# Small attention layers: v kept on the chip, first groups loaded during the in-projection, out-projection with tokens on partitions

## The reference

```python
# layer 0
x = x + _L0_attn_a_ref(_layernorm(x), Wq, Wk, Wv, Wo, W_down_kv, W_up_k, W_up_v)
    latent_kv = (x @ Wk + x @ Wv) @ W_down_kv
    qh, kh, vh = heads(x @ Wq), heads(latent_kv @ W_up_k), heads(latent_kv @ W_up_v)
    scores = clip(einsum('bhqd,bhkd->bhqk', qh, kh) * scale, -1e4, 1e4) * decay
    attn = softmax(clip(scores, -1e4, 1e4))
    return einsum('bhqk,bhkd->bhqd', attn, vh) (heads joined) @ Wo
# layer 4
x = x + _L1_attn_a_ref(_layernorm(x), Wqkv, Wout, Wpos, coeffs)
    logits = einsum('bihd,bjhd->bhij', q, k) * 8 ** -0.5 + pos_bias
    return einsum('bhij,bjhd->bihd', softmax(logits), v) (heads joined) @ Wout.T
```

## Time and profile before

| | us |
|---|---|
| runs, median of 3 (lowest to highest) | 4288.15 (4287.07 to 4292.68) |
| profiled execution, its own time | 4286.97 |
| span of the profiled execution | 4285.2 |
| layer 0: in-projection, attention, out-projection, statistics | 24.3 to 98.8, to 813.5, to 841.1, to 853.5 |
| layer 4: the same | 3004.6 to 3076.5, to 3644.8, to 3673.4, to 3685.7 |

### The profile page before, as it was taken

One profiled execution on the slowest core, in us unless ns is written; L12 is line 12 of the kernel. 1 busy time (PEld: TensorE's weight loads), 2 busy tenths in 40 slices (PEclk: granted clock), 3 DMA queues, 4 the chain that ended last, 5 costly groups with the idle time before them and its releaser, 6 DMA issues. The chain is left out here.

```text
span 4285.2 us, 58306 instructions
## 1 busy us (share of the span) xinstructions
PE 3440.0 (80%) x18432; PEld 2108.1 (49%) x18432; DVE 3112.8 (73%) x7125; ACT 2445.8 (57%) x4454; POOL 1239.0 (29%) x855
## 2 busy tenths in 40 slices
PE   5788888687946999999999978793499999657736
PEld 2455555365733555555555536572366666433314
DVE  3899999656864777777777745685388887569986
ACT  2788888535722656556565534572299999322203
POOL 0000000034421566666566654341000000025520
PEclk9899999878976999999999988896799999778868
DMA  5333332212436666666766611342634342100000
GB/s 184 60 62 62 62 51 35 37 42 102 143 97 81 86 87 89 85 85 87 90 85 86 84 23 46 112 142 67 189 45 61 60 64 31 26 18 8 5 29 26
DMA packets 285571, 303.79 MB, mean 71 GB/s; under 512 B 97951, under 2 KB 187487, under 8 KB 285140
## 3 DMA queue, kind: packets, MB, share of 16 engines
q1 hardware_dynamic: 275540, 279.07, 37.0%
q0 software_dynamic: 9728, 20.99, 1.4%
HBM read 122.30 MB, written 75.96 MB: 46 GB/s over the span
## 5 line engine op out<-in xcount | busy, mean ns | idle before, releaser
L1118 DVE TENSOR_REDUCE at_b_top<-ps 128x1 f32<-128x512 f32 x1024 | 661.9, 680 | 356.9 <-PE ps L878 356.2
L1007 ACT ACTIVATE at_b_e<-ps 128x512 f32<-128x512 f32 x1024 | 583.6, 598 | 474.2 <-PE ps L884 461.2
L550 ACT ACTIVATE at_a_e<-at_a_logits,at_a_neg_top 128x512 f32<-128x512 f32 x1024 | 656.1, 716 | 156.1 <-DVE at_a_neg_top L610 155.0
L777 POOL TENSOR_TENSOR at_b_e_pair<-at_b_e 128x1024 f32<-128x1024 f32 x256 | 603.8, 2380 | 402.5 <-PE ps L906 400.0
L474 PE MATMUL ps<-at_a_k,at_a_q 96*128 96x512 f32 x1024 | 476.3, 491 | 187.4 <-DVE at_a_clipped L578 118.3
L878 PE MATMUL ps<-at_b_k,at_b_q 96*128 96x512 f32 x1024 | 502.0, 494 | 40.2 <-DMA at_b_k<-at_b_k_hi 37.9
L543 ACT ACTIVATE at_a_eT<-ps 128x512 f32<-128x512 f32 x896 | 461.9, 589 | 0.4
L884 PE MATMUL ps<-at_b_q,at_b_k 98*128 98x512 f32 x1024 | 427.2, 418 | 19.0 <-ACT at_b_e L1007 18.6
L606 DVE CUSTOM_DVE_ANT_0 at_a_logits<-ps,at_a_strip 128x512 f32<-128x512 f32 x512 | 340.3, 688 | 110.7 <-issue 33.1
L474 PEld LDWEIGHTS ps<-at_a_k,at_a_q 96*128 96x128 f32 x1024 | 184.7, 190 | 399.8 <-DVE at_a_clipped L578 208.8
L578 DVE TENSOR_SCALAR at_a_clipped<-ps 128x512 f32<-128x512 f32 x512 | 351.2, 686 | 39.1 <-PE ps L474 38.0
(11 more groups left out here) (333 smaller groups left out, 6451.5 us busy)
## 6 DMA issues: line engine op xcount, KB each, us to landing
moe_stage<-in_moe_w SPq DMA_DIRECT2D x46, 768.0 KB
at_b_q<-at_b_q_hi SPq DMA_DIRECT2D x128, 256.0 KB, 5.2
at_b_k<-at_b_k_hi SPq DMA_DIRECT2D x128, 256.0 KB, 7.7
v<-in_a_va SPq DMA_DIRECT2D x64, 256.0 KB, 3.6
at_a_v<-v SPq DMA_DIRECT2D x64, 256.0 KB, 7.2
at_b_q<-at_b_q_lo SPq DMA_DIRECT2D x64, 256.0 KB, 7.6
at_b_k<-at_b_k_lo SPq DMA_DIRECT2D x64, 256.0 KB, 8.0
slot_rows<-empty_slots SPq DMA_DIRECT2D x44, 288.0 KB, 7.0
```

What stands on the lines that cost most here:

```text
L550: act.activation(e[:, j, qb, :], logits[:, j % 2, qb, :], ACT.Exp, bias=neg_top[:, j % 2, qb:qb + 1]).then_inc(exp_done, 1)
L777: pool.tensor_tensor(e_pair[:, j, :, :], e[r][:, j, 0:2, :], e[r][:, j, 2:4, :], ALU.add).then_inc(pair_done, 1)
L1007: act.activation(e[r][:, j, b, :], g.ps[:, ST_BANK + b % 2, :], ACT.Exp).then_inc(exp_done, 1)
L1118: dve.tensor_reduce(top[:, t, j, qb:qb + 1], g.ps[:, bank, :], AX_X, ALU.max).then_inc(max_done, 1)
```

## The change

- A new class `SmallBuffers` holds `q4`, `k4`, the decay strip or the bias strips, and a new `v_all` (v of all batches, 8 x 4 x 128 columns on each partition, unpadded). It lives across in-projection and attention. Its semaphores are not cleared.
- In-projection: `va` with its zeros and ones is gone; DVE copies v into `v_all`; SP stores no v. POOL zeroes `q4` and `k4` here. After the weights SP loads the decay strip (layer 0) or the four bias strips (layer 4). After the stores of batches 5 and 6 it loads the q and k pieces of attention groups 1 and 2.
- Attention: POOL sets the padding of the four `v4`, then copies, for each group, 16 x 8 columns of `v_all` into `v4` (once the product of the group four before is done). SP starts with the loads of group 3. The first bias strips aren't loaded here.
- Out-projection: a ring of four for o; w is loaded after the first batch's o; PE multiplies with the turned o as the stationary side, in four pieces, so that the result has tokens on partitions; the copy L1662 and the turn L1642 are gone. DVE takes `bn_stats` of batch n - 1 after the add of batch n. The phase is followed by a `row_stats` phase that only has the `bn_aggr` and the short steps, and the next layer's own is skipped.

```diff
+class SmallBuffers:
+    def __init__(self, nc, stack, sems, name, decay):
...
+        self.v_all = sb("v_all", [P, B, TB, DM])
+    def zero(self, pool):
+        for r in range(2):
+            pool.memset(self.q4[r][:].bitcast(F32), 0.0).then_inc(self.zeroed, 1)
+            pool.memset(self.k4[r][:].bitcast(F32), 0.0).then_inc(self.zeroed, 1)
+    def load_stacks(self, sp, g, r, batch, heads):
+        for row, dq, dk in ((0, g.q_hi8, g.k_hi8), (32, g.q_hi8, g.k_lo8), (64, g.q_lo8, g.k_hi8)):
+            for dst, src in ((self.q4[r], dq), (self.k4[r], dk)):
+                sp.dma_start(dst[row:row + 8].bitcast(F32),
...
 def project_small(nc, g, name, scale, latent, weights, ahead):
...
+            @block.gpsimd
+            def _(pool):
+                ahead.zero(pool)
...
+                if latent:
+                    sp.dma_start(ahead.decay_strip[:], g.decay).then_inc(ahead.decay_loaded, 16)
+                else:
+                    for j in range(HG):
+                        ahead.load_strip(sp, g, j, 0)
...
-                        sp.wait_ge(v_done, n)
-                        settle(sp, sp_settled)
-                        for hg in range(4):
-                            sp.dma_start(g.v8[bass.ds((n - 1) * 4 + hg, 1)].rearrange("a (t p) n -> p (a t) n", p=P),
...
+                        if n in (5, 6):
+                            if n == 5:
+                                sp.wait_ge(ahead.zeroed, 4)
+                            sp.wait_ge(stored[n % 2], 16 * 4)
+                            ahead.load_stacks(sp, g, n % 2, n - 5, 0)
...
-                for r in range(2):
-                    dve.memset(va[r][:], 0.0).then_inc(ones_set, 1)
-                dve.wait_ge(ones_set, 2)
-                for r in range(2):
-                    dve.memset(va[r][:, :, :, 8:9], 1.0).then_inc(ones_set, 1)
-                dve.wait_ge(ones_set, 4)
...
-                        dve.tensor_copy(va[r][:, :, :, 0:8], bank_v.rearrange("p (t h d) -> p t h d", t=TB, d=8)
+                        dve.tensor_copy(ahead.v_all[:, n - 1], bank_v.rearrange("p (t c) -> p t c", t=TB)
                                         ).then_inc(v_done, 1)
...
 def attend_small(nc, g, name, decay, ahead):
...
-                for r in range(2):
-                    pool.memset(q4[r][:].bitcast(F32), 0.0).then_inc(zeroed, 1)
-                    pool.memset(k4[r][:].bitcast(F32), 0.0).then_inc(zeroed, 1)
+                for r in range(4):
+                    pool.memset(v4[r][:], 0.0).then_inc(v_set, 1)
...
+                        wait(pool, pv_done, n - 4)
+                        pool.tensor_copy(v4[n % 4][:].rearrange("p t (h d) -> p t h d", d=32)[:, :, :, 0:8],
+                                         ahead.v_all[:, batch, :, heads * 32:heads * 32 + 32].rearrange(
+                                             "p t (h d) -> p t h d", d=8)).then_inc(v_spread, 1)
...
-                if decay:
-                    sp.dma_start(decay_strip[:], g.decay).then_inc(decay_loaded, 16)
-                sp.wait_ge(zeroed, 4)
...
-                        wait(sp, pv_done, n - 4)
-                        settle(sp, sp_settled)
-                        sp.dma_start(v4[rv][:], item(g.v8, batch * 4 + heads + 1).rearrange("a (t p) n -> p (a t) n", p=P)
-                                     ).then_inc(v_loaded[rv], 16)
-                        if not decay and st.c == 1:
+                        if n > 2:
+                            wait(sp, s_ready, 16 * (n - 2))
+                            ahead.load_stacks(sp, g, r, batch, heads)
+
+                        if not decay and st.c == 1 and st.i > 0:
...
-                                pe.wait_ge(v_loaded[st.slot(1, 4)], 16 * st.use(1, 4))
+                                pe.wait_ge(v_spread, st.n(1))
...
 def project_out(nc, g, name, w_out):
+    with nc.sbuf_tensor(f"{name}_stats", [P, TILES, 6], F32) as stats:
...
+                        wait(sp, t_ready, n - 4)
...
+                        if n == 1:
+                            sp.dma_start(w[:], w_out).then_inc(w_loaded, 16)
...
                         for tb in range(TB):
-                            ins = pe.transpose(g.ps[:, YT_BANK + r, tb * P:(tb + 1) * P],
-                                               yT[r][:, tb * P:(tb + 1) * P], g.ident[:])
-                        ins.then_inc(yt_ready, 1)
+                            cols = slice(tb * P, (tb + 1) * P)
+                            ins = pe.matmul(g.ps[:, Y_BANK + n % 2, cols], oT[n % 2][:, cols], w[:], start=True, stop=True)
+                        ins.then_inc(mm_done, 1)
...
+                    def take_stats(n):
+                        dve.wait_ge(added, n)
+                        for tile in range((n - 1) * TB, n * TB):
+                            dve.bn_stats(stats[:, tile, :], g.x_all[:, tile, :]).then_inc(stats_done, 1)
...
+                        dve.tensor_tensor(x, g.ps[:, Y_BANK + n % 2, :].rearrange("p (t d) -> p t d", t=TB), x, ALU.add
+                                          ).then_inc(added, 1)
+                        if n > 1:
+                            take_stats(n - 1)
+                    take_stats(B)
...
+        row_stats(nc, f"st_after_{name}", g.x_all, g.mean_var, g.rstd, 1e-5, stats)
+        g.stats_ready = True
```

More of the change, by code:

```diff
@@ L385, in attend_small @@
         o_tok = [ph.sb(f"o_tok{r}", [P, TB, HG, 8]) for r in range(2)]
-        zeroed, decay_loaded = ph.sem("zeroed"), ph.sem("decay_loaded")
-        loaded = [ph.sem(f"loaded{r}") for r in range(2)]
-        v_loaded = [ph.sem(f"v_loaded{r}") for r in range(4)]
+        v_set, v_spread = ph.sem("v_set"), ph.sem("v_spread")
         s_ready, logits_done, top_done = ph.sem("s_ready"), ph.sem("logits_done"), ph.sem("top_done")
@@ L399, in attend_small @@
         on_dve = () if decay else (3,)
-        strip_loaded = [] if decay else [ph.sem(f"strip_loaded{j}") for j in range(HG)]
         slots_zeroed, slots_numbered = ph.sem("slots_zeroed"), ph.sem("slots_numbered")
@@ L447, in step @@
[L447 to L448 removed]
+                                ahead.load_strip(sp, g, j, heads)
                     if decay and st.has(2) and st.n(2) <= SLOT_TILES:
@@ L1664, in _ @@
[L1664 to L1675 removed]
+                        act.activation(oT[n % 2][:], g.ps[:, T_BANK + n % 2, :], ACT.Copy).then_inc(t_read, 1)
```

177 lines of the change are left out of this document (83 added, 94 removed).

## The result

The changed kernel takes 4228.56 us (median of 4 runs, 4221.85 to 4230.05), the kernel before 4288.2 (4 runs, 4287.07 to 4292.68): a ratio of 0.9856, 95% interval 0.9839 to 0.9873. The forecast was 4228, range 4219 to 4241. The profiled execution went from 4286.97 to 4230.05, its span from 4285.2 to 4228.2: 57.0 less, where my sum had 59.7. The median fits better than the sum does, and so it has to be read term by term.

The account below looks back on a forecast made before the run. Attention groups run at DVE's pace in layer 0 and PE's in layer 4, so gains lie in phase heads and tails: 26.4 + 33.3 = 59.7 us off 4286.97 gives 4227.3, plus 1.2 makes 4228, range 4219 to 4241.

Parts of the forecast that it names:

- Start of attention, 15.9 / 17.1: Block start to DVE's first instruction: memsets and loads done beforehand, 1.2 us remain; gain 15.9 us layer 0, 17.1 layer 4.
- Rival 4: Start of attention: early loads land late or first group is slow, half of 33 us stays, 4245; chance 0.04.
- Tail of layer 0, 3.6: End of layer 0's in-projection: without v stores the k store is last, landing at 93.6 instead of 97.2; gain 3.6 us.
- Tail of layer 4, 6.4: End of layer 4's in-projection: without queued v issues the last stores land by 3068.5 instead of 3074.9; gain 6.4 us.
- Heads, 0.3 / 0.3: Start of each in-projection: DVE's memsets gone, POOL's beside normalising; middle taken, gain 0.3 us in each layer.
- two instructions per memset: In-projection heads: normalising is out after POOL's second memset; gain 1.9 us in layer 0, 2.3 in layer 4.
- Rival 1: In-projection heads: POOL's memsets hold DVE to the end, each loses 1.6 us instead of gaining 0.3, 4232; chance 0.25.
- Inside attention, -2: Layer 0's attention groups: POOL's 32 copies hold DVE 0.06 us each, a loss of 2 us; layer 4 none.
- Rivals 2 and 3: Layer 0 attention: POOL copies hold DVE in full, 10 us, 4236, chance 0.08; long copies make it slower, 4306, chance 0.02.
- Out-projection, 8.3 / 9.0: Out-projection: last transposes start sooner, bn_stats behind the barrier gone; gain 8.3 us in layer 0, 9.0 in layer 4.
- Body of the in-projection, 0: In-projection steps: chain PE, ACT, DVE unchanged, six early loads added and v stores dropped; cost nothing.
- rival 5: In-projection: stores hold its eight steps, so fewer stored bytes save 5 us per layer, 4218; chance 0.05.

Follow-up runs that it names:

- e2: Changed kernel, but the loads of the first two attention groups are issued in the attention again: 4234.92 us, ratio 0.9875.
- e3: Changed kernel with the early loads behind the stores of batches 3 and 4 instead of 5 and 6: 4224.9 us, ratio 0.985.
- p1: Changed kernel, each of the twelve early 64 KB loads filling 32 partitions instead of 8 (output wrong): 4220.11 us.
- e7: Changed kernel with eight o buffers in the out-projection instead of four: 4221.99 us.
- e1: Kernel before with only the new out-projection of the changed one: 4268.92 us against 4287.08, ratio 0.9958.
- b1: Changed kernel with early loads behind batches 3 and 4, eight o buffers, half the o loads issued by ACT between its copies: 4210.68 us, ratio 0.9834.
- e5: Changed kernel with POOL's copies of v cut to one head's 8 columns (output wrong): 4221.09 us, ratio 0.9861.
- e8: Changed kernel with eight o buffers and half the o loads issued by ACT, all ahead of its copies: 4222.3 us, ratio 0.9865.
- a2: Changed kernel measured again, no edit: 4218.74 us, ratio to before 0.9851.
- e4: Changed kernel, but POOL begins its four clears only when the first batch is normalised: 4223.17 us, ratio 0.9854.
- b2: Kernel b1 with, in addition, POOL's clears begun only when the first batch is normalised: 4213.09 us.

## Why the prediction came out as it did

- **Start of attention, 15.9 / 17.1:** right, 16.1 / 17.3. It was read off one stretch in which only POOL worked, and it is more than half of the gain. Rival 4 is out.
- **Tail of layer 0, 3.6:** right, 3.2. **Tail of layer 4, 6.4:** 2.7. The step "as in layer 0 ... land by 3068.5" failed. I had priced the early loads by SP's issue time and by "more than 10 us to land", asked what they would delay if they hung, and named the next stores, but then set the cost at nothing. They don't hang; they keep half of the engines busy at 51 to 66 GB/s, and the last store behind them lands 3.8 us later than without them (e2, e3, p1). With that removed the term is 6.5.
- **Heads, 0.3 / 0.3:** 1.9 / 2.05. The bound with two instructions per memset was the true one (1.9 and 2.3); I took the middle of two cases where row 853.51 had shown two passing. Normalising ended 3.8 us after the block's start, as that branch said. Rival 1 is out. The sentence that "the second batch ... has several us to spare" was wrong in layer 4: PE waits 1.27 us for it there in the kernel before and in the changed one, and 2.6 with the later clears.
- **Inside attention, -2:** no cost that can be told from the spread. The seeming agreement (-1.5) was chance. Rivals 2 and 3 are out by the kernel with four times the copies.
- **Out-projection, 8.3 / 9.0:** 5.7 / 7.4. Three steps. "Some 1.5 to 2 of these are waits for the ring of two and a weight load ahead of them that now stands behind the first four": the weight load still takes its 0.55 in the same queue, ahead of 28 loads; and a queue that takes one issue of 1.8 us where others take 0.5 does so with any ring (e7). So the last transposes started 0.4 us sooner relative to the block in layer 0 and 1.7 in layer 4, not 2. The hand-overs from there to the last `bn_stats`, summed to 4.5, took 5.2 (814.24 to 819.43): PE multiplies for batch 7 before batch 8. And bn_aggr begins 1.80 us behind the stats, not 1.06. Of these 0.7 us, 0.2 are that DVE reaches the barrier 0.27 us behind its last `bn_stats` and not 0.05 as behind the add, and 0.5 are SP's clears: they are 0.06 us apart (I had taken 0.05), but one of them comes 0.38 behind the one before. In e1 none does, and the gap is 1.34; why SP pauses stays open. Part of the whole shortfall is spread: in the nine profiles of kernels with this same out-projection it takes 27.5 to 28.3 / 26.5 to 27.5 us, a gain of 5.7 to 6.4 / 7.4 to 8.4, so 8.3 was too high by 1.9 at least and 9.0 by 0.6.
- **Body of the in-projection, 0:** right; rival 5, the stores as its bound, is out in both layers.
- **The sum:** 3.4 too low, 7.9 too high, the small terms 1.8 too low: 2.7 net. The changed kernel's second measurement, 4218.74, is just below the range's lower edge, with the kernel before at 4282.39 beside it; its ratio to before (0.9851) gives the same as the first (0.9856). What was right is the mechanism and the sign of each term but the one inside attention; that the median agreed with 4228 to 1 us is luck in part, since terms too high and terms too low cancel.

## What to carry to other kernels

A load that is moved under other work is priced by what it does to the transfers that share its engines and not by its issue: look at how many partitions it fills, and at how long the next stores take to land. When a queue of DMA issues sets the pace, sum all its issues and see what is queued behind them on the engine that issues them, before changing buffers. And a measured difference of one term that fits the forecast is no proof of it: amplify the suspected cost and look whether it grows.

## What the runs showed of the hardware

- A load of 64 KB into 8 partitions shares the DMA engines badly: 0.54 busy at 51 to 66 GB/s, and 256 KB stores behind it land in up to 8.1 us instead of 2.7 (k_lo of batch 7 in layer 4: issued 3031.22, landed 3039.27). The same bytes into 32 partitions delayed nothing.
- Two DVE instructions of 128 columns pass with each POOL memset, though the next memset is queued already, and they end 0.08 to 0.15 us behind it. In the other direction POOL's copy stands for 0.55 us behind the DVE instruction with two SBUF inputs and not at all beside one with a single one (0.28 to 0.30 us in layer 4), and four times as many copies left DVE's mean at 681 ns (680 without copies).
- The granted clock in layer 4's in-projection is not a constant of the code. By windows of 1 us it rose to 2.4 GHz 3.4 us behind PE's first instruction in the kernel before and 2.7 us in e3, but 7.2 us in the changed kernel and 7.9 in its second profile, whose head is that of e3. Later one or two of the steps took 7.95 us instead of 6.30, with the clock between 0.7 and 0.9 in their windows. The body took 53.6 to 53.8 us with an early rise and two slow steps (before, e1, e3, b1) or a late rise and one (changed), 55.4 to 55.8 with a late rise and two (e2, e5 to e8, a2, p1), and 56.7 and 56.9 in e4 and b2. This spread of 2 us is as large as most of the terms in dispute.
